# Attention values on four quarter tiles of TensorE, and a slot order that opens with the scores

## The reference

```python
for i in range(DEPTH):                                    # 6
    x = attn_layer(shift_tokens(x), Wqkv[i], q_scale[i], k_scale[i], Wo[i]) + x
    x = ffn_layer(shift_tokens(x), ln_g[i], ln_b[i], W1[i], b1[i], W2[i], b2[i]) + x

# attn_layer: q, k, v = x @ Wqkv; l2norm of q and k; rotary with scale; then windows of 32 tokens:
#   each window of queries sees its own window of keys and the one before it (64 keys)
sim = jnp.einsum('bhwie,bhwje->bhwij', bq, bk2) * QK_SCALE
attn = jax.nn.softmax(jnp.where(mask, -big, sim), -1)
out = jnp.einsum('bhwij,bhwje->bhwie', attn, bv2)         # then @ Wo
```

## Time and profile before

| what | value |
|---|---|
| runs, us | 1661.52, 1663.18, 1662.98; median 1662.98 |
| profiled execution, us | 1662.44; span from first to last instruction 1660.6 |
| mean granted clock | 0.983 of full speed |
| PE, PEld busy | 1581.1 us (95%), 1210.2 us (73%) |
| DVE busy | 1471.4 us (89%) |
| ACT busy | 1430.6 us (86%) |
| POOL busy | 1313.8 us (79%) |
| DMA | 66.39 MB, mean 40 GB/s |

### The profile page before, as it was taken

One profiled execution on the slowest core, in us unless ns is written; L12 is line 12 of the kernel. 1 busy time (PEld: TensorE's weight loads), 2 busy tenths in 40 slices (PEclk: granted clock), 3 DMA queues, 4 the chain that ended last, 5 costly groups with the idle time before them and its releaser, 6 DMA issues.

```text
span 1660.6 us, 68799 instructions
## 1 busy us (share of the span) xinstructions
PE 1581.1 (95%) x25860; PEld 1210.2 (73%) x25860; DVE 1471.4 (89%) x3011; ACT 1430.6 (86%) x2851; POOL 1313.8 (79%) x1305
## 2 busy tenths in 40 slices
PE   7879999999999999999999999999999999999995
PEld 5657777777777777777777777777777777777773
DVE  4499999999999999999999999999999999999874
ACT  4267998998999899899889989989998999999985
POOL 6188888888888888888888888888888888778855
PEclk9799999999999999999999999999999999999997
DMA  4111111111111111111111111111111101110100
GB/s 138 51 39 40 41 34 38 32 46 37 46 38 32 38 38 43 44 40 33 32 38 44 46 42 32 33 32 51 40 43 38 32 28 41 40 33 27 32 22 26
DMA packets 41425, 66.39 MB, mean 40 GB/s; under 512 B 7072, under 2 KB 16032, under 8 KB 41376
## 3 DMA queue, kind: packets, MB, share of 16 engines
q1 hardware_dynamic: 40224, 65.38, 13.2%
q10 hardware_dynamic: 1152, 0.34, 0.1%
HBM read 20.61 MB, written 1.05 MB: 13 GB/s over the span
## 4 chain that ended last, share of the span: by engine, by line
PE 58%; DVE 26%; issue 12%; ACT 2%; DVEq 1%; DMA 0%; POOL 0%; ACTq 0%; POOLq 0%
PE ps_s L539 13%; PE ps_a L539 11%; PE ps_qk L539 10%; PE ps_f L539 8%; PE ps_po L539 7%; DVE qk_rot L1269 5%; PE ps_v L539 5%; DVE qk L1267 4%; PE ps_po L658 4%; DVE ssq L1275 4%; DVE row_sum L1311 3%; DVE row_max L1302 3%; DVE prob L1305 2%; PE ps_f L747 1%; DVE xc L1324 1%
## 5 line engine op out<-in xcount | busy, mean ns | idle before, releaser
L436 POOL TENSOR_TENSOR qk<-qk,rnorm 128x512 f32<-128x512 f32 x384 | 393.0, 1044 | 132.1 <-DVE rnorm L1295 123.3
L428 POOL TENSOR_TENSOR qk<-qk,qk_rot 128x512 f32<-128x512 f32 x384 | 484.4, 1283 | 0.0
L443 POOL TENSOR_TENSOR prob<-prob,row_inv 128x512 f32<-128x512 f32 x192 | 200.4, 1044 | 115.5 <-DVE row_inv L1314 115.5
L1275 DVE TENSOR_REDUCE ssq<-squares 128x8 f32<-128x512 f32 x384 | 260.4, 678 | 3.4 <-ACT squares L959 3.4
L1267 DVE TENSOR_TENSOR qk<-ps_qk,table 128x512 f32<-128x512 f32 x384 | 262.2, 683 | 1.1
L1269 DVE TENSOR_TENSOR qk_rot<-ps_qk,table 128x512 f32<-128x512 f32 x384 | 260.7, 679 | 0.0
L959 ACT ACTIVATE squares<-ps_qk 128x512 f32<-128x512 f32 x384 | 232.1, 604 | 11.5 <-PE ps_qk L539 3.8
L953 ACT COPY p_bd<-ps_po 64x512 f32<-64x512 f32 x378 | 217.1, 574 | 21.0 <-PE ps_po L658 18.7
L539 PEld LDWEIGHTS ps_s<-ident,qk 128*128 128x128 f32 x1528 | 170.9, 140 | 77.6 <-DVE prob L1305 64.1
L539 PE MATMUL ps_s<-ident,qk 128*128 128x128 f32 x1528 | 202.9, 276 | 23.8 <-DVE prob L1305 22.9
L539 PE MATMUL ps_qk<-w_hi,xs_hi 128*128 (+1 forms) x384 | 188.7, 491 | 12.9 <-DVE qk_rot L1269 6.8
(11 more groups left out here) (207 smaller groups left out, 3490.4 us busy)
## 6 DMA issues: line engine op xcount, KB each, us to landing
v_back<-v_own SPq DMA_DIRECT2D x192, 192.0 KB, 2.4
w_raw<-in_wqkv SPq DMA_DIRECT2D x48, 192.0 KB, 2.4
v_back<-v_own SPq DMA_DIRECT2D x96, 64.0 KB, 2.1
wo_sb<-in_wo SPq DMA_DIRECT2D x12, 256.0 KB, 3.0
w_sb<-in_w SPq DMA_DIRECT2D x6, 341.0 KB, 3.0
w_sb<-in_w SPq DMA_DIRECT2D x6, 192.0 KB, 2.5
x_in<-in_x SPq DMA_DIRECT2D x4, 256.0 KB, 4.7
out<-s_out SPq DMA_DIRECT2D x8, 128.0 KB, 1.9
```

Of the source, the lines that this page charges most:

```text
L428: nc.gpsimd.tensor_tensor(qk[:, s, i, :], qk[:, s, i, :], qk_rot[:, s, i, :], ALU.add).then_inc(added, 1)
L436: nc.gpsimd.tensor_tensor(heads(qk[:, s, i, :]), heads(qk[:, s, i, :]), rnorm[:, s, 8 * i:8 * i + 8].unsqueeze(2).to_broadcast([P, 8, HEAD ...
L443: nc.gpsimd.tensor_tensor(heads(prob[:, s, :]), heads(prob[:, s, :]), row_inv[:, s, :].unsqueeze(2).to_broadcast([P, 8, HEAD]), ALU.mult). ...
L1275: V.tensor_reduce(ssq[:, s, 8 * i:8 * i + 8], heads(squares[:, s, OCTET * i:OCTET * i + OCTET]), AX, ALU.add).then_inc(ssq_done, 1)
```

## The change

It does these things; all else stays as it was.

1. `keep_p` makes one copy of the turned probabilities, 128 x 512, into a plain tile p_t. The tile p_bd and POOL's memset of it are gone.
2. `values` makes 32 products of 64x64 array tiles in place of 16 of 128x64. Each takes 64 partitions (the keys of one half, `later`) of v and of p_t, and moves 32 columns. The column half of the array is `head`, the row half is `later`. The two row halves write to two different banks.
3. These two banks are ps_po and ps_q (the left half of each). ps_v, ps_po, ps_q and ps_k become four neighbouring banks for it. So `values` waits until DVE has read the queries (`q_scaled`, u + 5), and the next slot's projection of q waits until ACT has copied the attention (`attn_copied`).
4. In PE's body the slot opens with `scores`; the projection of q comes after it.
5. `keep_attention` reads the two banks in one copy of the same size.
6. The drain, written out by hand, uses other bank pairs and has its waits moved to match.

```diff
-            nc.gpsimd.memset(p_bd[:], 0.0)
...
-            def values(u, n, j, s, ps=ps_po):
+            def values(u, n, j, s):
+
+                pe.wait_ge(q_scaled, u + 5)
+                values_into(valued, u, n, j, s)
+
+            def values_into(area, u, n, j, s):
 
                 pe.wait_ge(p_turned, u + 1)
                 pe.wait_ge(v_shifted[j], (n + 1) * (32 if j % 2 else 16))
+                nc.tensor.sem_inc(pe_passed, 1)
                 for c in range(PAIRS):
                     for odd in range(2):
+                        v = v_own if odd else v_back
                         for head in range(2):
-                            v = v_own if odd else v_back
-                            o = ps[64 * head:64 * head + 64, P * c:P * c + P].rearrange(
-                                "p (h o q) -> p h o q", h=2, o=2)[:, :, odd, :]
-                            last = mm(o, v[:, j, 64 * (2 * c + head):64 * (2 * c + head) + 64],
-                                      p_bd[:, s, 8 * head + 4 * (c // 2) + 2 * odd + c % 2].rearrange("p a b -> p (a b)"), True, True,
-                                      skip_group_check=True)
+                            for later in range(2):
+                                rows = slice(64 * later, 64 * later + 64)
+                                to = 64 * c + WINDOW * odd
+                                at = P * (2 * head + c // 2) + 64 * odd + WINDOW * (c % 2)
+                                last = mm(area[64 * head:64 * head + 64, later, to:to + WINDOW],
+                                          v[rows, j, 64 * (2 * c + head):64 * (2 * c + head) + 64],
+                                          p_t[rows, s, at:at + WINDOW], True, True, skip_group_check=True)
                 last.then_inc(o_done, 1)
...
             def body(n):
                 for j in range(UNITS):
                     u = UNITS * n + j
-                    project(n, j, 0, ps_q, q_scaled, q_done)
                     if live(u - 3):
                         scores(u - 3, (j - 3) % UNITS, (j - 3) % 2)
+                    if live(u - 5):
+                        wait(pe, attn_copied, u - 4)
+                    project(n, j, 0, ps_q, q_scaled, q_done)
                     if live(u - 4):
                         turn_p(u - 4, j % 2)
...
             def keep_p(u, s, ps=ps_po):
                 wait(act, o_done, u - 1)
                 act.wait_ge(pt_done, u + 1)
-                for h in range(2):
-                    rows = slice(64 * h, 64 * h + 64)
-                    last = copy(p_bd[rows, s, :, h, :], ps[rows, :].rearrange("p (g q) -> p g q", q=WINDOW))
-                last.then_inc(p_turned, 1)
+                copy(p_t[:, s, :], ps[:]).then_inc(p_turned, 1)
...
-            def keep_attention(u, m, j, ps=ps_po):
+            def keep_attention(u, m, j, area=valued):
...
+                copy(attn_t[:, PAIRS * octet:PAIRS * octet + PAIRS, 1 + P * tile:1 + P * tile + P].rearrange(
+                    "p c (g t) -> p g c t", g=2), area.rearrange("p g (c t) -> p g c t", t=64)).then_inc(attn_copied, 1)
```

More of the change, by code:

```diff
@@ L70, in bank, with banks @@
             return ctx.enter_context(nc.psum_tensor(name, [P, 512], F32))
-        def bank_pair(name):
-            return ctx.enter_context(nc.psum_tensor(name, [P, 2, 512], F32))
+        def banks(name, n):
+            return ctx.enter_context(nc.psum_tensor(name, [P, n, 512], F32))
         def sem(name):
@@ L112, in build @@
         prob = sb("prob", [P, 2, OCTET])
-        p_bd = sb("p_bd", [P, 2, PAIRS * 4, 2, WINDOW])
+        p_t = sb("p_t", [P, 2, OCTET])
         row_max = sb("row_max", [P, 2, 8])
@@ L149, in build @@
         w1_early = [staged[l % 2][:, 2 * FF * (l // 2):2 * FF * (l // 2 + 1)] for l in range(DEPTH)]
-        ps_qk, ps_s = bank_pair("ps_qk"), bank_pair("ps_s")
-        ps_q, ps_k, ps_qs, ps_tk = ps_qk[:, 0, :], ps_qk[:, 1, :], ps_s[:, 0, :], ps_s[:, 1, :]
-        ps_v, ps_po, ps_a, ps_f = (bank(n) for n in ("ps_v", "ps_po", "ps_a", "ps_f"))
+        ps_vpqk, ps_s = banks("ps_vpqk", 4), banks("ps_s", 2)
+        ps_v, ps_po, ps_q, ps_k = (ps_vpqk[:, i, :] for i in range(4))
+        ps_vp, ps_pq, ps_qk = (ps_vpqk[:, i:i + 2, :] for i in range(3))
+        ps_qs, ps_tk = (ps_s[:, i, :] for i in range(2))
+        ps_a, ps_f = (bank(n) for n in ("ps_a", "ps_f"))
         def scored(pair):
             return pair[:, :, 0:OCTET // 2]
+        valued = scored(ps_pq)
         x_loaded = [sem(f"x_loaded_{p}") for p in range(TWOS)]
@@ L650, in turn_into, with turn_p @@
                 last.then_inc(done, 1)
-            def turn_p(u, s, ps=ps_po):
-                if ps is ps_po:
+            def turn_p(u, s, ps=ps_po, turning=True):
+                if turning:
                     wait(pe, attn_copied, u)
@@ L835, in drain @@
                 pe.wait_ge(q_scaled, END)
+                pe.wait_ge(attn_copied, a)
                 turn_into(ps_q, c, 0, 0)
@@ L844, in drain @@
                 scores(c, 2, 0, ps_qk, False)
-                values(a, LAST, 0, 0)
+                pe.wait_ge(v_copied, END)
+                values_into(scored(ps_vp), a, LAST, 0, 0)
                 ln_spread(LAST - 2, END, STEPS + BATCHES - 4)
-                pe.wait_ge(v_copied, END)
-                turn_p(b, 1, ps_v)
                 ln_mean(LAST - 1)
                 scores(d, 3, 1, ps_s, False)
+                pe.wait_ge(attn_copied, a + 1)
+                turn_p(b, 1, ps_v, False)
                 ff_up(LAST - 2, 0)
-                pe.wait_ge(attn_copied, a + 1)
-                values(b, LAST, 1, 1)
+                values_into(scored(ps_vp), b, LAST, 1, 1)
                 ln_variance(LAST - 1)
                 ff_up(LAST - 2, 1)
-                turn_p(c, 0, ps_v)
+                pe.wait_ge(attn_copied, b + 1)
+                turn_p(c, 0, ps_v, False)
                 ff_up(LAST - 2, 2)
                 pe.wait_ge(sub_done, c + 1)
-                values(c, LAST, 2, 0, ps_k)
+                values_into(scored(ps_qk), c, LAST, 2, 0)
                 out_projection(LAST, 0)
-                turn_p(d, 1, ps_v)
+                turn_p(d, 1, ps_v, False)
                 ln_spread(LAST - 1, END + 1)
                 pe.wait_ge(sub_done, END)
+                pe.wait_ge(attn_copied, c + 1)
                 up_into(ps_q, LAST - 1, 0)
@@ L866, in drain @@
                 up_into(ps_f, LAST - 1, 2)
-                values(d, LAST, 3, 1)
-                down_into(ps_v, LAST - 3)
+                values_into(scored(ps_vp), d, LAST, 3, 1)
+                down_into(ps_k, LAST - 3)
                 out_projection(LAST, 1)
-                down_into(ps_k, LAST - 2)
+                down_into(ps_v, LAST - 2)
                 ln_mean(LAST)
@@ L1011, in keep_attention @@
                 act.wait_ge(o_done, u + 1)
-                copy(attn_t[:, PAIRS * octet:PAIRS * octet + PAIRS, 1 + P * tile:1 + P * tile + P],
-                     ps[:].rearrange("p (c t) -> p c t", t=P)).then_inc(attn_copied, 1)
+                copy(attn_t[:, PAIRS * octet:PAIRS * octet + PAIRS, 1 + P * tile:1 + P * tile + P].rearrange(
+                    "p c (g t) -> p g c t", g=2), area.rearrange("p g (c t) -> p g c t", t=64)).then_inc(attn_copied, 1)
             def ln_square(m):
@@ L1107, in drain @@
                 keep_turned_k(d, 3, ps_tk)
-                keep_attention(a, LAST, 0)
+                keep_attention(a, LAST, 0, scored(ps_vp))
                 softmax_exp(c, 0)
@@ L1113, in drain @@
                 softmax_exp(d, 1)
-                keep_attention(b, LAST, 1)
+                keep_attention(b, LAST, 1, scored(ps_vp))
                 up_from(ps_f, LAST - 2, 1, ff_pairs[1])
@@ L1120, in drain @@
                 keep_p(d, 1, ps_v)
[L1121 removed]
+                keep_attention(c, LAST, 2, scored(ps_qk))
                 up_from(ps_f, LAST - 2, 2, ff_pairs[1])
                 gelu_spare(LAST - 2, ff_pairs[1][1])
[L1124 removed]
+                keep_attention(d, LAST, 3, scored(ps_vp))
                 up_from(ps_q, LAST - 1, 0, ff_pairs[2])
@@ L1423, in drain @@
                 silu_invert(2)
-                after_ff(LAST - 3, ps_v)
+                after_ff(LAST - 3, ps_k)
                 after_attention(LAST)
                 ln_center(LAST)
-                after_ff(LAST - 2, ps_k)
+                after_ff(LAST - 2, ps_v)
                 ln_var(LAST)
```

2 lines of the change are left out of this document (removed).

## The result

The changed kernel takes 1739.96 us, median of 4 runs (1738.52 to 1741.19), against 1663.08 us of the kernel before, measured beside it (4 runs, 1661.52 to 1672.42). The ratio is 1.0461, 95% interval 1.0434 to 1.0487: 77 us slower. Forecast were 1709 us, 46 slower. The profiled execution took 1740.81 us, its span is 1739.0.

What follows compares the result with a forecast made beforehand. The prediction took a ring through PE, ScalarE and DVE to bound the kernel; its period rises from 32.21 to 33.29 us, 43 x 1.08 = 46.4 us on 1662.4, giving 1709 us. Range: 1653 to 1732, likeliest case 1690 to 1730.

Steps and rivals of the forecast that it cites:

- The ring: Cycle through PE, ScalarE and DVE setting the period: 13.78 + 3.40 + 14.97 + 0.06 = 32.21 us, going to 33.29.
- DVE's leg: DVE's work from `rn_a` in slot 1 to the end of slot 3's subtraction, 14.97 us of the period.
- Values load-bound: Weight loads, not moved columns, pace the values block on PE, so quarter tiles leave its time unchanged.
- The rivals of cheaper values: Cheaper values: 1653 us with PE the bound (faster case, chance 0.13), or 1663 to 1690, including a shorter DVE leg (0.17).
- the shared load path: Row halves cannot load side by side: +0.93 us a values block, 1812 us; chance 0.07 together with other stalls above 1730.
- The four times of the prediction: Skill page's speedup, cited as up to four times where both dimensions are at most 64, supporting the cheaper-values rival.
- Changeovers: PE switching array tiling: +0.13 us each before values in slots 3 and 0, -0.09 where scores follow values directly.
- The new waits: Values wait for q's rotation in slots 1 (0.85 us) and 2; projection's wait for the attention copy hidden; no cost beyond the ring.
- 1.08 us later: Slot 1's query projection on PE starts at 840.96 against 839.88, lengthening each of 43 periods by 1.08 us.
- Drain and first four steps unchanged, 3 us either way: The kernel's drain and its first four steps, without table reload yet, keep their time within 3 us.
- a little lost on that supply: PE's instructions per step rise from 1096 by 256; a small supply loss would take the forecast to some 1725 us.
- the scores' branch: Path to `rn_a` in slot 1 through scores, row maximum and subtraction, claimed as long as the query path, without slack.

Runs made afterwards that it cites:

- The first experiment: Changed kernel with slot 1's exponential table reload moved ahead of the squares of q: 1694.55 us, ratio 1.0185.
- the written-out steps: PE's steps 5 to 14 written out instead of looped: in the changed kernel 1744.03 us, ratio 1.0476; in the kernel before 1661.05 us, ratio 0.9992.
- the order alone: Kernel before with only the scores put ahead of the query projection in each slot: 1704.69 us, ratio 1.0245.
- the table out of the ring: Kernel before with the exponential table reload moved from slot 1 to right behind GELU in slot 0: 1656.68 us, ratio 0.9954.

## Why the prediction was off: point by point

- **The ring, and which way it goes: right.** `rn_a` waits 1.80 us once a step (forecast 1.8), the row maximum waits no more, squares to `rn_a` is unchanged, DVE's leg is 14.98 (14.97), as long as forecast. The first experiment shows it: 45 us come back when the table load starts ahead of the squares.
- **Values load-bound: right.** The block holds PE for 1.06 against 1.03 (the forecast's sum kept 1.04; its sign, 0.93 to 1.0, was a little low), with 64 recorded products for 32 and half the columns moved. A load takes 135 ns (137 and 138 in the kernel before, on 128 rows), and doubling the loads at the same columns gives 2.05. The rivals of cheaper values (1653 and 1663 to 1690) fall. So does the shared load path (1812): one block of its kind would have shown 1.9. The Trainium skill's page "TensorEngine Tiling (Array Packing)", section Theoretical Speedup, gives up to two times for one dimension of at most 64. The four times of the prediction are this figure taken twice, and the kernel before, with its tiles of 128x64, had already taken it once. Of the other factor of two nothing is seen here: the time per block did not fall at all, since the loads, not the moved columns, set it.

The group of loads of the kernel after (count, busy us, mean ns), beside 138 of the earlier trace rows:

```profile
L542 PEld LDWEIGHTS ps_vpqk<-p_t,v_back 64*64 64x64 f32 x6144 | 171.9, 135 | 154.8 <-issue 154.7
```

- **Changeovers: right in sum.** 0.09 and 0.10 in slots 3 and 0 for the 0.13 forecast; between the spread and the scores 0.36 (847.99 to 848.35) for 0.30.
- **The new waits: right.** Values wait for q's rotation in slots 1 and 2 (1.09 and 0.77; 0.85 and about 0.5 forecast); the attention copy is hidden. As forecast, two ways from slot 2's rotation to the next turn of q are level: PE's own through values, scores and projections (863.06 to 867.61, 4.55, forecast 4.56), and DVE's, whose subtraction ends at 867.53. So the waits add nothing, but the one in slot 2 has no slack: the trace's chain of what ended last goes through these values.
- **"1.08 us later": the term that failed.** The query projection came 1.52 later. What was left out is the edge of PE's loop. The forecast took the gap from values to the next block, and the one from scores to projection, from the loop of before, as if they belonged to the blocks. By the written-out steps the edge costs 0.20 us a period before and 0.70 after. With the edge out of both kernels the change costs 33.06 - 32.00 = 1.06 us a period: the forecast's 1.08. This is no luck of the sum: its parts agree as well, the values' start in slot 3 (0.09 for 0.13), the scores' block (0.79) and the way to slot 0's values (0.10 for 0.13). With the edge the change costs 1.56, and 0.5 x 41 is 20 of the 31 us missed; most of the rest are the first steps. The new order has only a small part in the dearer edge: with the order alone values to scores are 1.07, where the block itself holds PE for 1.03, and scores to projection 1.03 for 0.79, together about 0.3. The other 0.4 come with the tiles: 64 short products in front, behind which the sequencer reaches the branch 0.33 later, and one instruction more for the new wait. The forecast counted blocks and waits of PE, and not the instructions of its sequencer between them.
- **"Drain and first four steps unchanged, 3 us either way": failed.** The first six intervals grew by 13.7 us, 2.2 of them forecast. The order alone makes 2.0 of the 13.7 (209.1 against 207.1). Stops in mid-block make 5.0: four stand in the third to fifth intervals of the kernel after (0.35, 1.35, 1.65 and 1.64 us), none in the kernel before. The written-out steps show the cause with everything else equal: steps that run once must read their instructions, the change gives PE 24% more of them a step, and PE then stops in mid-block; the profiled execution lost about 1.3 us a step by it, the kernel before nothing. The forecast had the larger count before it, and priced it only as "a little lost on that supply", as a case of up to 1725. The second interval grew most, by 5.4 us, and has no such stop. Its windows (as in the earlier trace rows; the third figure from the end is the granted clock), the kernel before first:

```profile
95.00:123.20 28.20, 22.51 (x435) 16.64 (x433) 27.58 (x53) 21.77 (x47) 24.58 (x24) 1.00 0.14 42
```

```profile
94.60:128.10 33.50, 25.80 (x535) 21.42 (x536) 30.18 (x62) 21.45 (x46) 24.75 (x24) 0.85 0.13 36
```

The granted clock was 0.85 of full speed in it. With the same written-out code it took 31.1 us at 0.95 in the kernel with written-out steps. So some 2.5 us of these 5.4 were not there again with the same code, and what makes the other 3 stays open.
- **The side claim that the scores' branch was as long:** nearly. With the table out of the ring `rn_a` came 0.2 us earlier.

The balance: 41 x 1.06 = 43.5 us as forecast and 41 x 0.5 = 20.5 for the loop's edge, together 64 where the trace has 62.8; 13.7 in the first six intervals. That is 76.5 measured; the two profiled executions are 78.4 apart, the rest stands ahead of the first interval and behind the last.

## What to carry to other kernels

Where an engine's work comes in a loop, look for what stands on both sides of the loop's edge: behind long instructions its branch and waits were hidden here, behind many short ones they showed. Splitting a block into twice as many short products made the edge dearer than moving a block across it did. When a change multiplies an engine's instructions, count them per step: the 24% more cost nothing inside this loop apart from its edge, stopped PE in some of the steps that run once, and with 69% more (1906 for 1128) the loop itself had to be read again in every round. Before swapping two blocks to shorten one path through a ring, write down the other path through the same slot; here the cheap move was a table load, worth 0.4%, and not the order of the blocks.

## What the runs showed of the hardware that was not expected

- A loop whose body has 1394 recorded PE instructions a step is read once (0.66 MB of instructions in all); with 1906 it is read anew in every round (6.93 MB), the branch takes 3.9 us in place of 0.21, and a step 48 us in place of 33.8. Where between them the limit lies was not tried.
- Code that runs once keeps up at 1128 recorded PE instructions in 32.0 us, and does not always at 1394 in 33.1: stops of 0.4 to 2.2 us in some of the steps.
- The edge of PE's loop cost 0.20 us a period in the kernel before, about 0.3 with the new order alone, and 0.70 with the quarter tiles and their waits as well. The branch took 0.21 in each; what differed is how much of it and of the register and wait instructions, some 0.1 us each, was hidden behind products.
- Moving half the columns on quarter tiles of 64x64 saved nothing: 1.03 to 1.06 us a block, at the same number of loads for each part of the array.
